# Two zero products a slot on TensorE, between the value products and the transposes of a two-layer attention kernel

## The chip, the cores and the metric

The kernel runs on one core of one Trainium2 chip. The metric is device time in microseconds (us), the median of several executions; lower is better.

## What is computed

The reference is two transformer blocks, one behind the other, on `x` of 8 batches, 128 tokens and 128 channels, all in float32. Each block has self-attention, cross-attention with a context `ctx_768` (8 x 128 x 96) and an MLP with four times 128 hidden channels; every one of the six sub-blocks starts with a layer norm that is scaled and shifted by the condition vector, and ends with a residual sum. The first block has 16 heads of 64 channels with rotary embedding. The second, where the change lies, has 16 heads of 8 channels:

```python
def _attend(q, k, v):
    sim = jnp.einsum('bhid,bhjd->bhij', q, k) * HD ** (-0.5)
    attn = jax.nn.softmax(sim, axis=-1)
    out = jnp.einsum('bhij,bhjd->bhid', attn, v)
    return out.transpose(0, 2, 1, 3).reshape(out.shape[0], -1, D)
...
h1 = _modulate(_ln(x), sh_msa, sc_msa)
...
x = x + (out @ W_proj + b_proj)
```

## The kernel before

Each engine has a program of its own, written out by hand, and the engines meet at counted semaphores. The order of instructions on each engine is the order of the code; there is no scheduler. SBUF tensors are allocated once, and PSUM is used as eight fixed banks of 128 x 512 float32: `S[0]`, `S[1]` and `X` (scores, in turn), `T[0]` and `T[1]` (transposed probabilities), `Y`, `W` (norm transposes, projections, sums) and `O` (value products).

Work is cut into items. An item is two heads of four batches (a half), so that one bank holds four 128 x 128 squares. A layer has 4 runs (self-attention of half 0 and 1, cross-attention of half 0 and 1) of 8 items, so 32 items. The first layer runs as slots -2 to 31 of `l0_slot`, the second as slots 0 to 39 of `l1_slot`, one item a slot, in a software pipeline that spans three slots. Every engine has a function of the same name with its own part of each slot. In slot s of the second layer:

- TensorE computes the scores of item s (`score1`, line 873 by way of the helper `mm`, shown as `bank<-km,q`: eight products with 32 rows of weights), then the value products of item s-2 (`prob_values1`, `bank<-swp,vst`), then transposes the probabilities of item s-1 into `T[0]` and `T[1]` (`transpose_probs1`, line 1139, `bank<-small,raw`), then does what `background1` has for the slot: `turn_back` (line 1170), `attention_T` (line 1176), `project_attention`, `transpose_norm` (line 884), or parts of the MLP. `score1` of slot s waits for the exponentials of the first head of item s-1.
- VectorE takes the row maxima (line 772) of both heads, copies `T[0]` to SBUF (line 777), and does statistics, sums and divisions.
- ScalarE computes the exponentials (line 506), four instructions a head, and between the two heads copies `T[1]` (line 512); in every fourth slot it also copies `O` (line 516).
- GpSimd masks keys and does part of the layer norms.

In slots 8, 16 and 24 a new run begins: there TensorE does the value products and transposes first, and the scores only after the projection of the new queries. In slots 12, 20 and 28 `project_attention` adds the attention's output, which VectorE then adds to `x`.

`keep_warm(count, dst)` issues `count` products of `idle`, a 128 x 512 bf16 tensor that VectorE sets to zero at the start, into the bank `dst`. Before the change it is called twice, ahead of the first layer, with 11 and 8 products. A product of it has 128 x 128 weights and 512 columns, and no semaphore.

Of the kernel before, what the change touches and what calls it, by code (L numbers as in the profile page):

```python
# [52 lines left out]
def place(s):  # L53

    return s // (2 * RUN), s // RUN % 2, s % RUN


def build(nc, small_in, x_in, ctx_in, ctxT_in, wqkv_in, wo_in, wmod_in, wsq_in, wff_in, row_in, out):
    es = ExitStack()
    with es:  # L60
# [64 lines left out]
        S, T, X, Y, O, W = bank[0:2], bank[2:4], bank[4], bank[5], bank[6], bank[7]  # L125
# [13 lines left out]
        def bcols(u):  # L139
            return slice(u * P, (u + 1) * P)  # L140
# [730 lines left out]
        def _(pe):  # L871
            def mm(o, lhsT, rhs, start, stop):
                return nc.tensor.matmul(o, lhsT, rhs, start=start, stop=stop, skip_group_check=True)  # L873

            def keep_warm(count, dst):
                for _ in range(count):
                    mm(dst[:, :], idle[:, 0:P], idle[:, :], True, True)
# [69 lines left out]
            def transpose_probs(s, hh):  # L947
                pe.wait_ge(norms[hh], s + 1)
                if s:
                    pe.wait_ge(copied[hh], s)  # L950
                if hh:
                    pe.wait_ge(v_out, min(s + 3, ITEMS))
                    if s == 28:
                        pe.wait_ge(gelu_done, FF)
                    if s == 31:
                        pe.wait_ge(vst_out[0], 1)
                for u in range(HALF):
                    last = nc.tensor.transpose(T[hh][:, bcols(u)], prob[:, hh, bcols(u)], ident)  # L958
                last.then_inc(probs_T[hh], 1)

            def prob_values(s):
                for hh in range(2):
                    pe.wait_ge(copied[hh], s + 1)
                if s:
                    pe.wait_ge(o_out, s)
                if s == 1:
                    wait_hT(0, 1)
                if s in (4, 5):
                    pe.wait_ge(ctx_h, s - 3)
                if 6 <= s <= 11:  # L970
                    pe.wait_ge(proj_out, s - 5)
                if s in (12, 20):
                    wait_hT(1, s // RUN - 1)
                if s == 13:
                    pe.wait_ge(mod_read, 2)
                if s == 27:
                    wait_hT(2, 0)
                if s == 28:
                    pe.wait_ge(x_sum[0], 3)
                for u in range(HALF):  # L980
                    for hh in range(2):
                        last = mm(O[DH0 * hh:DH0 * (hh + 1), bcols(u)],
                                  v0[:, s % 4, u * P + DH0 * hh:u * P + DH0 * (hh + 1)], probT[:, s % 2, hh, bcols(u)],
                                  True, True)
                last.then_inc(pv, 1)

            def project_out(s):
                a, half, n = place(s)
                if n == 0:
                    if s:  # L990
                        run = s // RUN - 1
                        pe.wait_ge(x_sum[run % 2], run // 2 + 1)
                    seed("ca_bo" if a else "sa_bo", W)
                    pe.wait_ge(ld_wo[a], 16)
                pe.wait_ge(o_out, s + 1)
                for u in range(HALF):
                    last = mm(W[:, bcols(u)], oT[:, s % 2, bcols(u)], wo[:, a * RUN + n, :], False, False)
                last.then_inc(wo_done, 1)

            def project_values(half):  # L1000
                dst = (T[1], Y)[half]
                if half:
                    pe.wait_ge(proj_out, AT["q", 1] + 1)
                else:
                    pe.wait_ge(copied[1], 31)
                for u in range(HALF):
                    last = mm(dst[:, bcols(u)], hT[:, half, bcols(u)], wsq[:, SQ["v"] * P:(SQ["v"] + 1) * P], True, True)
                last.then_inc(proj_v, 1)

            def project(what, half):  # L1010
                i = AT[what, half]
                dst = PROJ_BANK[i]
                if i == 0:
                    pe.wait_ge(ld_sq, 16)
                    pe.wait_ge(ld_ctxT, 16)
                if what in ("ck", "cv"):
                    pe.wait_ge(proj_out, AT["ctx1", half] + 1)
                if what == "q":
                    wait_hT(3, half)
                if what == "cq":  # L1020
                    wait_hT(4, half)
                weights = wsq[0:DC if what == "ctx1" else P, SQ["ctx" if what == "ctx1" else what] * P:][:, 0:P]
                src = {"ctx1": ctxT, "ck": ctx1T, "cv": ctx1T}.get(what, hT)
                if what == "cv":
                    for u in range(HALF):
                        last = mm(dst[:, bcols(u)], src[:, half, bcols(u)], weights, True, True)
                else:
                    last = mm(dst[:, :], weights, src[:, half, :], True, True)
                last.then_inc(proj, 1)
# [83 lines left out]
            def score1(s):  # L1113
                a, half, n = place(s)
                j = n // 2
                if n == 0:
                    pe.wait_ge(proj_out, AT["cq" if a else "q", half] + 1)
                    pe.wait_ge(km_first[half], a + 1)
                elif n % 2 == 0:
                    pe.wait_ge(km_rest[half], (SLOTS - 1) * a + j)  # L1120
                if s >= 1:
                    pe.wait_ge(exps1[0], s)
                if s >= 2:
                    pe.wait_ge(exps1[1], s - 1)
                for u in range(HALF):
                    for hh in range(2):
                        g = (2 * n + hh) % GROUPS
                        lanes = slice(GR * g, GR * (g + 1))
                        ins = mm(SB[(2 * s + hh) % 3][:, bcols(u)], q1[lanes, half, bcols(u)], km[lanes, half, j, bcols(u)],
                                 True, True)  # L1130
                        if u == HALF - 1:
                            ins.then_inc(scores1[hh], 1)

            def transpose_probs1(s, hh):
                pe.wait_ge(exps1[hh], s + 1)
                if s:
                    pe.wait_ge(copied1[hh], s)
                for u in range(HALF):
                    last = nc.tensor.transpose(T[hh][:, bcols(u)], prob1[:, s % 2, hh, bcols(u)], ident)  # L1139
                last.then_inc(probs_T1[hh], 1)  # L1140

            def prob_values1(s):
                a, half, n = place(s)
                for hh in range(2):
                    pe.wait_ge(copied1[hh], s + 1)
                if n == 0:
                    pe.wait_ge(vst_out[half], a + 1)
                if s == 0:
                    pe.wait_ge(o_out, ITEMS)
                if s % 4 == 0 and s:  # L1150
                    pe.wait_ge(os_out, s // 4)
                for u in range(HALF):
                    for hh in range(2):
                        c = (u * H + 2 * n + hh) * VW
                        last = mm(O[VW * u:VW * (u + 1), bcols(s % 4)], vst[:, half, c:c + VW], probT1[:, s % 2, hh, bcols(u)],
                                  hh == 0, hh == 1)
                last.then_inc(pv1, 1)
# [35 lines left out]
            def l1_slot(s):  # L1193
                first = s in (RUN, 2 * RUN, 3 * RUN)
                if s < ITEMS and not first:
                    score1(s)
                if s == 0:
                    transpose_probs(ITEMS - 1, 1)
                    project_out(ITEMS - 2)
                    prob_values(ITEMS - 1)  # L1200
                if first and s > RUN:
                    project("cq", s // RUN - 2)
                if 2 <= s <= ITEMS + 1:
                    prob_values1(s - 2)
                if 1 <= s <= ITEMS:
                    transpose_probs1(s - 1, 0)
                    transpose_probs1(s - 1, 1)
                if s == RUN:
                    project("q", 1)
                    project("k", 1)  # L1210
                if first:
                    score1(s)
                if s == RUN:
                    project_values(1)
                background1(s)
# [129 lines left out]
```

## Time and profile before

| | us |
|---|---|
| median of 3 runs | 428.16 (425.07 to 430.17) |
| profiled execution, its own time | 422.87 |
| its span, first to last instruction | 420.7 |
| TensorE busy | 383.0 |
| VectorE busy | 312.4 |
| ScalarE busy | 303.6 |
| GpSimd busy | 165.6 |
| TensorE's mean granted clock | 0.984 of full |

The time of an execution is 2.17 us more than its span. The second layer's slots begin at about 262 us and its last slots, which are MLP work, end with the span. "Busy" for TensorE comes from records whose ends are modelled, so the start times of its instructions are read rather than their ends. A float32 product of 128 x 128 shows as two records, a transpose as one. The granted clock is a share of 2.4 GHz; 0.50 is the lower of its two levels, 1.2 GHz, and a value between is a stretch that has some of both.

### The profile page before, as it was taken

The page shows a single profiled execution, that of the slowest core. Times are in us where ns is not written, and L with a number is a line of the kernel's source. Part 1 is how long each engine was busy: PE and PEld are TensorE (multiplying, and loading weights), DVE is VectorE, ACT ScalarE, POOL GpSimd, SP SyncE. Part 2 cuts the span into 40 slices and gives each one's busy share as a digit, 9 for nine tenths or more (in the row PEclk, how much of TensorE's full clock was granted, in tenths as well). Part 3 has the DMA queues.
Part 4 walks back from the last instruction along what each step waited for, and adds up shares of the span by engine and source line. Part 5 has one row for each costly group of instructions (what it writes and reads, how often), then busy time and mean ns, then how long its engine had stood idle before and what let it go on. Part 6 is the DMA issues. An engine that isn't in the chain of part 4 may idle for free. (4 is left out here: it accounts for less than half of the span.)

```text
span 420.7 us, 9918 instructions
## 1 busy us (share of the span) xinstructions
PE 383.0 (91%) x3599; PEld 288.5 (69%) x3599; DVE 312.4 (74%) x677; ACT 303.6 (72%) x1042; POOL 165.6 (39%) x159
## 2 busy tenths in 40 slices
PE   7778989999999999999999989899798898898976
PEld 3446767777877777777767577777586686687554
DVE  4699898988887999988999477764567567567430
ACT  2376777886885878787868947797698778688722
POOL 4578593523643443733346241321473402002020
PEclk9899999999999999999999999999999989989989
DMA  6334424232252121212221010000000000000000
GB/s 189 119 131 127 157 89 163 83 115 96 74 191 107 64 89 68 85 63 90 75 77 68 34 51 2 2 2 0 2 2 2 3 2 2 2 2 2 2 25 26
DMA packets 16036, 26.11 MB, mean 62 GB/s; under 512 B 3614, under 2 KB 6308, under 8 KB 15860
## 3 DMA queue, kind: packets, MB, share of 16 engines
q1 hardware_dynamic: 13572, 18.43, 12.2%
q0 software_dynamic: 1696, 6.16, 5.1%
q10 hardware_dynamic: 720, 0.87, 0.7%
q8 instruction: 30, 0.49, 0.5%
q14 instruction: 18, 0.15, 0.1%
HBM read 8.15 MB, written 0.52 MB: 21 GB/s over the span
## 5 line engine op out<-in xcount | busy, mean ns | idle before, releaser
L281 POOL TENSOR_TENSOR swp<-swp,small 128x512 f32<-128x512 f32 x64 | 82.0, 1293 | 108.2 <-PE bank L873 76.5
L411 ACT ACTIVATE prob<-bank,nmax 128x128 f32<-128x128 f32 x256 | 91.5, 391 | 4.8 <-DVE nmax L668 4.8
L506 ACT ACTIVATE raw<-bank,nmax 128x128 f32<-128x128 f32 x256 | 73.5, 391 | 20.1 <-DVE nmax L772 20.1
L772 DVE TENSOR_REDUCE nmax<-bank 128x4 f32<-128x512 f32 x64 | 41.2, 686 | 26.5 <-PE bank L873 26.3
L411 ACT ACTIVATION_READ_ACCUMULATOR prob<-bank,nmax 128x1 f32 x256 | 59.3, 231 | 0.0
L668 DVE TENSOR_REDUCE nmax<-bank 128x4 f32<-128x512 f32 x64 | 41.2, 685 | 17.7 <-PE bank L873 17.6
L222 POOL TENSOR_TENSOR rstd<-vare,neg_half 128x4 f32<-128x4 f32 x12 | 12.4, 1034 | 104.5 <-DVE vare L613 104.4
L675 DVE TENSOR_TENSOR prob<-prob,rz 128x512 f32<-128x512 f32 x64 | 49.9, 780 | 2.2
L873 PE MATMUL bank<-hT,wqkv 128*128 128x512 f32 x96 | 50.0, 606 | 1.1 <-ACT hT L394 1.1
L417 ACT ACTIVATE probT<-bank 128x512 f32<-128x512 f32 x32 | 19.1, 597 | 40.4 <-PE bank L958 40.4
L873 PE MATMUL bank<-km,q 32*128 32x128 f32 x512 | 37.5, 284 | 10.7 <-ACT raw L506 6.1
L958 PEld LDWEIGHTS bank<-small,prob 128*128 128x128 f32 x256 | 28.8, 140 | 25.9 <-DVE prob L675 15.7
L691 DVE TENSOR_TENSOR qk<-qk,swp 128x512 f32<-128x512 f32 x64 | 44.4, 733 | 2.4 <-issue 1.2
L958 PE MATMUL bank<-small,prob 128*128 128x128 f32 x256 | 40.5, 280 | 4.4 <-DVE prob L675 4.1
L685 DVE TENSOR_TENSOR qk<-bank,small 128x512 f32<-128x512 f32 x64 | 43.6, 681 | 1.0 <-ACT raw L402 0.9
L873 PEld LDWEIGHTS bank<-km,q 32*128 32x128 f32 x512 | 31.5, 187 | 17.8 <-ACT raw L506 7.6
L873 PE MATMUL bank<-qk 64*128 64x128 f32 x512 | 37.9, 288 | 5.9 <-DVE qk L691 5.9
L402 ACT ACTIVATE raw<-bank 128x512 f32<-128x512 f32 x64 | 40.7, 636 | 2.5 <-PE bank L873 2.5
L873 PEld LDWEIGHTS bank<-wo,oT 128*128 128x128 f32 x256 | 32.9, 191 | 13.0 <-issue 11.9
L873 PEld LDWEIGHTS bank<-qk 64*128 64x128 f32 x512 | 31.8, 190 | 12.1 <-DVE qk L691 6.9
L873 PE MATMUL bank<-probT,v 128*64 128x128 f32 x512 | 35.0, 278 | 3.9 <-ACT hT L394 1.8
L1139 PE MATMUL bank<-small,raw 128*128 128x128 f32 x256 | 36.9, 289 | 0.1
(112 smaller groups left out, 649.3 us busy)
## 6 DMA issues: line engine op xcount, KB each, us to landing
swp<-raw SPq DMA_DIRECT2D x128, 128.0 KB, 2.1
wqkv<-in_wqkv POOLq DMA_DIRECT2D x13, 192.0 KB, 3.0
wo<-in_wo POOLq DMA_DIRECT2D x2, 512.0 KB, 5.1
wff<-in_wff POOLq DMA_DIRECT2D x1, 1024.0 KB, 5.6
wsq<-in_wsq POOLq DMA_DIRECT2D x1, 576.0 KB, 6.2
x<-in_x SPq DMA_DIRECT2D x2, 256.0 KB, 4.6
wmod<-in_wmod POOLq DMA_DIRECT2D x1, 512.0 KB, 4.2
out_x<-x SPq DMA_DIRECT2D x2, 256.0 KB, 2.3
```

What stands on the lines that cost most here:

```text
L281: nc.gpsimd.tensor_tensor(four(swp[:, m % 2, f, :]), four(swp[:, m % 2, f, :]), sin[f], ALU.mult).then_inc(rope_sin[f], 1)
L402: nc.scalar.activation(raw[:, m % 2, f, :], (X, Y)[f][:, :], ACT.Copy).then_inc(raw_out[f], 1)
L411: last = nc.scalar.activation(prob[:, hh, bcols(u)], S[hh][:, bcols(u)], ACT.Exp, bias=nmax[:, s % 2, hh, u:u + 1], accum_out=zsum[:, s % ...
L506: last = nc.scalar.activation(prob1[:, s % 2, hh, bcols(u)], SB[(2 * s + hh) % 3][:, bcols(u)], ACT.Exp, bias=nmax[:, s % 2, hh, u:u + 1])
L668: nc.vector.tensor_reduce(nmax[:, s % 2, hh, :], four(S[hh][:, :]), AX.X, ALU.max, negate=True).then_inc(rowmax[hh], 1)
L675: nc.vector.tensor_tensor(four(prob[:, hh, :]), four(prob[:, hh, :]), rz[:, s % 2, hh, :].unsqueeze(2).broadcast_to([P, HALF, P]), ALU.mul ...
L685: nc.vector.tensor_tensor(four(qk[:, m % 2, f, :]), four((X, Y)[f][:, :]), cos[f], ALU.mult).then_inc(rope_cos[f], 1)
L691: nc.vector.tensor_tensor(qk[:, m % 2, f, :], qk[:, m % 2, f, :], swp[:, m % 2, f, :], ALU.add).then_inc(roped[f], 1)
L772: nc.vector.tensor_reduce(nmax[:, s % 2, hh, :], four(SB[(2 * s + hh) % 3][:, :]), AX.X, ALU.max, negate=True).then_inc(rowmax1[hh], 1)
L873: return nc.tensor.matmul(o, lhsT, rhs, start=start, stop=stop, skip_group_check=True)
L958: last = nc.tensor.transpose(T[hh][:, bcols(u)], prob[:, hh, bcols(u)], ident)
L1139: last = nc.tensor.transpose(T[hh][:, bcols(u)], prob1[:, s % 2, hh, bcols(u)], ident)
```

## The change

Slots 2 to 33 of the second layer get one more line on TensorE:

```diff
@@ -1202,6 +1202,7 @@
                     project("cq", s // RUN - 2)
                 if 2 <= s <= ITEMS + 1:
                     prob_values1(s - 2)
+                    keep_warm(2, T[0])
                 if 1 <= s <= ITEMS:
                     transpose_probs1(s - 1, 0)
                     transpose_probs1(s - 1, 1)
```

That is 32 calls and 64 products. They write `T[0]`, whose last content has been copied by then, since `prob_values1(s - 2)` in front of them waits for that copy; the transposes behind them overwrite it. No wait and no semaphore is added, and no other engine's program changes.

TensorE in slots 10 and 11 before (`bank<-km,q` are scores, `bank<-swp,vst` value products, L1139 the transposes of probabilities, L1170 `turn_back`, L1176 `attention_T`):

```order
L873 MATMUL bank<-km,q 128x128 x8
L873 MATMUL bank<-swp,vst 32x128 x8
L1139 MATMUL bank<-small,raw 128x128 x8
L1170 MATMUL bank<-small,oS 128x128 x4
L873 MATMUL bank<-km,q 128x128 x8
L873 MATMUL bank<-swp,vst 32x128 x8
L1139 MATMUL bank<-small,raw 128x128 x8
L1176 MATMUL bank<-small,xn 128x128 x4
```

The same two slots on TensorE now:

```order
L873 MATMUL bank<-km,q 128x128 x8
L873 MATMUL bank<-swp,vst 32x128 x8
L873 MATMUL bank<-idle 128x512 x2
L1139 MATMUL bank<-small,raw 128x128 x8
L1170 MATMUL bank<-small,oS 128x128 x4
L873 MATMUL bank<-km,q 128x128 x8
L873 MATMUL bank<-swp,vst 32x128 x8
L873 MATMUL bank<-idle 128x512 x2
L1139 MATMUL bank<-small,raw 128x128 x8
L1176 MATMUL bank<-small,xn 128x128 x4
```

The transposes and all that follows them in the slot stand behind two more products; the scores of the next slot too.

TensorE at the start of a run, slots 15 to 17, before (`bank<-hT,wsq` is the projection of the new queries; the x16 are the scores of slots 16 and 17):

```order
L1170 MATMUL bank<-small,oS 128x128 x4
L873 MATMUL bank<-hT,wsq 128x512
L873 MATMUL bank<-swp,vst 32x128 x8
L1139 MATMUL bank<-small,raw 128x128 x8
L873 MATMUL bank<-km,q 128x128 x16
L873 MATMUL bank<-swp,vst 32x128 x8
L1139 MATMUL bank<-small,raw 128x128 x8
```

And now:

```order
L1170 MATMUL bank<-small,oS 128x128 x4
L873 MATMUL bank<-hT,wsq 128x512
L873 MATMUL bank<-swp,vst 32x128 x8
L873 MATMUL bank<-idle 128x512 x2
L1139 MATMUL bank<-small,raw 128x128 x8
L873 MATMUL bank<-km,q 128x128 x16
L873 MATMUL bank<-swp,vst 32x128 x8
L873 MATMUL bank<-idle 128x512 x2
L1139 MATMUL bank<-small,raw 128x128 x8
```

Between the scores of slot 16 and those of slot 17 stands nothing, as before.

## Rows read from the trace of the kernel before

**Rows 1.** The page: TensorE's busy time, and the clock granted in 40 slices.

```profile
PE 383.0 (91%) x3599; PEld 288.5 (69%) x3599; DVE 312.4 (74%) x677; ACT 303.6 (72%) x1042; POOL 165.6 (39%) x159
...
PEclk9899999999999999999999999999999989989989
```

**Rows 2.** The chain that ended last, stretches of slots 9 to 13: start, us, what.

```profile
306.84 1.02 PE bank L1139 x8
307.87 0.38 issue
308.25 1.75 PE bank L873 x32
```

**Rows 3.** Windows: stretch and length, busy us (instructions) by engine, PEclk, DMA, GB/s.

```profile
305.09:308.25 3.16, 2.78 (x41) 2.25 (x41) 1.89 (x3) 2.77 (x11) 3.16 (x3) 1.00 0.00 0
308.25:311.39 3.14, 3.14 (x45) 2.65 (x45) 1.91 (x3) 3.14 (x11) 3.14 (x3) 1.00 0.02 5
326.44:332.06 5.62, 5.62 (x71) 4.18 (x71) 3.79 (x9) 4.34 (x14) 4.73 (x4) 1.00 0.02 6
332.06:335.17 3.11, 1.16 (x17) 0.97 (x16) 1.65 (x3) 1.79 (x6) 0.00 (x0) 1.00 0.00 0
335.17:339.24 4.07, 4.07 (x41) 3.19 (x41) 1.98 (x3) 2.13 (x8) 0.74 (x2) 0.62 0.00 0
339.24:342.63 3.39, 3.36 (x45) 2.84 (x45) 1.98 (x3) 3.29 (x11) 0.00 (x0) 0.95 0.02 5
366.01:370.18 4.17, 4.17 (x41) 3.23 (x41) 1.98 (x3) 2.12 (x8) 0.00 (x0) 0.61 0.00 0
```

**Rows 4.** Timeline of TensorE, slot 10: start, us, operation, count [idle before].

```profile
308.25 1.16 PE L873 MATMUL bank<-km,q 32*128 32x128 f32 x16 [0.38 <-issue]
309.33 0.67 PE L873 MATMUL bank<-swp,vst 128*32 128x128 f32 x16
309.93 1.09 PE L1139 MATMUL bank<-small,raw 128*128 128x128 f32 x8
310.86 0.60 PE L1170 MATMUL bank<-small,oS 128*128 128x128 f32 x4
```

**Rows 5.** Timeline of ScalarE and VectorE, slot 10.

```profile
308.97 2.30 ACT L506 ACTIVATE raw<-bank,nmax 128x128 f32<-128x128 f32 x8
309.41 1.29 DVE L772 TENSOR_REDUCE nmax<-bank 128x4 f32<-128x512 f32 x2 [1.24 <-PE bank L873]
```

**Rows 6.** Timeline of TensorE: the groups of the second layer that begin after a wait.

```profile
273.05 1.16 PE L873 MATMUL bank<-km,q 32*128 32x128 f32 x16 [0.88 <-ACT raw L506]
276.18 0.63 PE L884 MATMUL bank<-small,xn 128*128 128x128 f32 x4 [0.36 <-DVE xn L621]
293.34 1.16 PE L873 MATMUL bank<-km,q 32*128 32x128 f32 x16 [0.45 <-ACT raw L506]
322.37 1.16 PE L873 MATMUL bank<-km,q 32*128 32x128 f32 x16 [0.93 <-issue]
325.88 0.63 PE L884 MATMUL bank<-small,xn 128*128 128x128 f32 x4 [0.73 <-DVE xn L621]
335.17 1.20 PE L873 MATMUL bank<-km,q 32*128 32x128 f32 x16 [1.95 <-ACT raw L506]
356.71 0.63 PE L884 MATMUL bank<-small,xn 128*128 128x128 f32 x4 [0.33 <-DVE xn L621]
391.91 0.67 PE L873 MATMUL bank<-swp,vst 128*32 128x128 f32 x16 [0.48 <-ACT swp L512]
```

**Rows 7.** Timeline of TensorE: bf16 products of 512 columns, and what follows one.

```profile
5.90 1.89 PE L873 MATMUL bank<-idle 128*128 128x512 bf16 x8
...
317.26 0.38 PE L873 MATMUL bank<-parts_row,ones 3*128 3x512 bf16 x1
317.57 1.16 PE L873 MATMUL bank<-wsq,oT 128*128 128x128 f32 x8
```

**Rows 8.** The tile `idle`: weight loads and products, shortest/median/longest in ns.

```profile
L873 PEld LDWEIGHTS bank<-idle x19: 95/117/181, 1.3 to 7.2; 128*128 128x128 bf16 x19
L873 PE MATMUL bank<-idle x19: 376/380/634, 1.3 to 7.4; 128*128 128x512 bf16 x19
```

## The prediction

> **What bounds the kernel now.** I read the page first: TensorE is busy 91% of the span, and its clock is nearly always full [rows 1]. That says little of one stage, so I went to the second layer's slots, from 262 us on, the only ones that change: the chain of waits, then TensorE's timeline with the waits ahead of each group, then windows cut at the starts of the scores.
>
> A plain slot takes 3.14 to 3.16 us, and two things come out alike in it. In slot 9 (305.09 to 308.25) TensorE has scores, value products and transposes, 2.78 us of work, and then waits 0.38 us [rows 2, 3]: here a loop sets the pace (scores 1.1 us, row maximum of the first head half of 1.29, its exponentials half of 2.30 [rows 4, 5]; with handovers about 3.1 us), since the next scores need those exponentials. In slot 10 four transposes of `turn_back` are added, and TensorE runs from one score to the next without a wait, 3.14 us, scores, values, transposes, `turn_back` each starting where the former's pace allows [rows 3, 4]. ScalarE is full in that slot as well, 3.14 us. So wherever a slot has anything beside its three standing groups, TensorE's queue is the path; where it has not, or where VectorE's sum and statistics hold back the row maxima, TensorE waits.
>
> **The change part by part.** Nothing is removed, no wait is added, no transfer moves. Added are 64 bf16 products of 512 columns.
>
> Price of a pair. The zero products ahead of the first layer are the same instruction. The eight at 5.90 us take 1.89 us, of which the last takes 0.38, so the seven steps between starts are (1.89 - 0.38) / 7 = 0.216 us each at full clock [rows 7, 8]. The 0.117 us weight load of each [rows 8] is inside that step. A pair is 0.43 us. The value products before and the transposes behind are separated by a changeover already; I take it to be paid once, as now. The other end: a lone bf16 product in this layer, the seed of a sum, delays what follows by 317.57 - 317.26 = 0.31 us [rows 7]; two such are 0.62. Below 0.43 a pair can't go at this clock, since products don't overlap in these rows, but its effect on the path can, down to zero, where TensorE waits afterwards. I take 0.43, from the row that shows the very instruction.
>
> Now slot by slot, by the wait that follows the pair [rows 6]:
> - Full price, 18 slots. TensorE runs without a wait behind the pair: 4 and 5 (MLP work), 8 (projections), 10 to 12, 15 and 16 (326.44 to 332.06 is 5.62 us of 5.62 busy [rows 3]), 18 to 20, 23 and 24, 26 to 28, 32 and 33 (MLP work again). 18 x 0.432 = 7.78 us.
> - Slots 9, 17, 25: the wait of 0.38 us takes the pair but for 0.05: 0.15 us.
> - Slots 3 and 7 wait 0.36 us for normalised rows before their norm transpose, which leaves 0.07 each: 0.14. Slots 22 and 30 wait 0.33 there, and leave 0.10 each: 0.20.
> - Slot 31: 0.48 us of wait for ScalarE's copy of the transposes, which the pair itself makes later. Between 0 and 0.43, I take 0.20.
> - Nothing in slots 2 (0.88 of wait), 6 (0.45), 13, 21, 29 (0.93, behind VectorE's residual sum and statistics) and 14 (0.73). If that cover were gone it would be 6 x 0.43 = 2.6 us.
>
> Sum 7.78 + 0.15 + 0.14 + 0.20 + 0.20 = 8.47 us. The transposes are 0.43 later in every slot, and with them ScalarE's copy, which sits between its two heads' exponentials. In slot 10 it would push the second head by a few tenths, but the next scores are later too, by 0.43, so ScalarE isn't the end of the path there.
>
> Ends of the sum. Low: TensorE's ends are modelled, and ScalarE is full in slot 10. If ScalarE were the true bound in the six slots like it (10, 11, 18, 19, 26, 27), the pair would cost nothing there: 8.47 - 2.59 = 5.9 us. High: a pair of 0.62 is 18 x 0.62 = 11.2, plus 2.4 in the others by the same waits, 13.6 us.
>
> The clock. It fell twice in this layer. Scores of slot 17 came 1.95 us after TensorE went idle [rows 6], and from them on the clock shows 0.62 and then 0.95 [rows 3], so it was at the 1.2 GHz level for most of a slot; the same at 366.01. The two slots took 4.07 and 3.39 us where 3.14 is the pace at full clock: 0.93 + 0.25 = 1.18 us; at 366.01 it is 1.03 + 0.25 = 1.28, so 2.4 us together. Do the pairs mend that? They stand before the transposes, and the wait lies between the scores of slot 16 and of slot 17, with nothing of the change in it. It stays as long as it is, so I expect falls as before, and count zero for the clock. A fall that comes with the pairs in place costs a little more, since they run at half speed too.
>
> The Trainium skill ("TensorE: Matmul & The Clock Gate", "A second HAM failure mode: psum-queue depth-cycling") holds that many short idles between groups of products can make the clock swing. By that rule filling TensorE's time anywhere would help. The trace speaks against it here: slots with waits of 0.38 us kept 1.00, and the fall came behind the one wait of 1.95 us. By the rule the sum would lose the 2.4 us of both falls; by the rows it loses nothing.
>
> **Against which time.** The profiled execution took 422.87 us, so its sum is 431.3. The runs had a median of 428.16, 5.3 us more, from 425.07 to 430.17. What they lose over the profiled one I can't see. The added work is the same in both, so I put the forecast at 428.16 + 8.47 = 436.6 us, 2.0% slower. A measurement of this kernel tells about 1% (4.3 us) from no change.
>
> **Rivals.**
> 1. The clock is what the pairs buy, in part. The four or so slots around a fall have more busy time, and both falls go: 436.6 - 2.4 = 434.2 us. For it: the falls are next to pairs. Against: the wait itself stays. 13%.
> 2. Faster or even, by the same clock but at a larger size. If the 5.3 us by which the runs exceed the profiled execution were falls in this layer too (four or five at 1.2), the pairs would do away with them all: -2.4 - 5.3 = -7.7 us, against 5.9 to 8.5 us of added work: 426.4 to 429.0 us. It decides from some seven falls a run on (8.47 / 1.2); the profile has two in the layer. For it: the runs vary by 5 us, as a clock would make them. Against: the falls would have to be where a pair reaches. 7%, and 4% for beyond 1% faster.
> 3. ScalarE bounds more than TensorE: 5.9 us of cost, 434.1 us. For it: 3.14 us busy of 3.14. Against: TensorE's starts follow each other without a wait in the same slots, and slots 15 and 16, with 5.62 us of 5.62, have ScalarE at 4.34 [rows 3]. 10%.
> 4. A pair costs as the seed product does, 0.62: 441.8 us. For it: changing between column-tiled products, bf16 and float32 has a price that eight equal products don't show. 12%.
> 5. The pairs don't delay at all since TensorE could run ahead. Its queue is in order, and the transposes that follow have their inputs long before; nothing speaks for it. Under 1%.
>
> **How the numbers follow.** Forecast 58%, rivals 13, 7, 10 and 12%. Its own range is 433 to 440. The whole range reaches from rival 3 with part of rival 1 (5.9 - 2.4 = 3.5, 431.7 us), less a microsecond for the scatter of a median, to rival 4: 430.5 to 441.5. Faster by over 1% 4% (rival 2's far end); within 1% (up to 432.4) 14%, from the rest of rival 2, and where rivals 1 and 3 meet; slower by over 1% 82%.
>
> **What would show it.** In the changed profile: 64 more bf16 products of `idle` with 0.216 us between the two of a pair; slots 10 to 12 at about 3.57 us instead of 3.14, back to back; slot 9 at 3.2; slots 13 and 14 as long as now; the stretch of slots 15 and 16 at 6.5 instead of 5.62; a wait of about 1.95 us still ahead of slot 17's scores, and some of these waits still followed by a clock of 0.5 to 0.6. A run of eight slots would be some 2.3 us longer. I would be wrong if slots 10 to 12 keep 3.14 us (rival 3), if more than 0.5 us lies between the last value product and the first transpose beyond what lies there now (rival 4), or if the layer shows fewer falls of the clock and a time under 432 (rivals 1, 2).

## The result, and the profile after

| | before | changed |
|---|---|---|
| median of 20 runs each, us | 427.03 | 430.39 |
| lowest to highest, us | 421.03 to 430.17 | 426.58 to 434.49 |
| ratio, 95% interval | | 1.0125 (1.0087 to 1.0163) |
| profiled execution: span, us | 420.7 | 429.5 |

The change makes the kernel slower, by 1.25% in the ratio (5.3 us) and by 3.4 us between the medians. The ratio leaves out the longest runs of either kernel as disturbed; since in the kernel before these are mostly the runs with the lowest clock, and the clock is part of the question, I use medians, means over all runs and the trace beside it. The two profiled spans differ by 8.8 us, more than either: 2.07 of it are there before the second layer's third slot (269.39 us before, 271.46 after), in code that is the same in both. That part is scatter: the same slot begins at 270.31 us in a second trace of the kernel before and at 269.06 in a second one of the changed kernel.

The page of the changed kernel, the two rows that answer to [rows 1]:

```profile
PE 392.2 (91%) x3646; PEld 294.9 (69%) x3663; DVE 316.0 (74%) x677; ACT 305.6 (71%) x1042; POOL 165.2 (38%) x159
...
PEclk9889999999999999999999999999999999999999
```

TensorE is busy 9.2 us more, 91% again. The low clocks have moved: more of them in slices 2 and 3, in the first layer, fewer later.

Windows of the changed kernel, cut at the scores as in [rows 3]: slots 9, 10, 11, 12, then 15 with 16's transposes, the wait ahead of slot 17, slots 17, 18, and 25.

```profile
308.36:311.51 3.15, 2.99 (x41) 2.44 (x43) 1.68 (x3) 2.66 (x10) 3.15 (x3) 1.00 0.00 0
311.51:315.24 3.73, 3.61 (x48) 2.89 (x47) 2.29 (x4) 3.48 (x11) 3.73 (x3) 1.00 0.02 4
315.24:318.77 3.53, 3.37 (x47) 2.85 (x47) 2.83 (x6) 2.77 (x10) 1.29 (x3) 1.00 0.00 0
318.77:323.27 4.50, 4.50 (x53) 3.47 (x52) 1.98 (x3) 4.31 (x15) 0.00 (x0) 1.00 0.01 4
...
331.03:337.43 6.40, 6.24 (x74) 4.57 (x74) 3.88 (x9) 4.72 (x16) 4.73 (x4) 1.00 0.02 5
337.43:340.54 3.11, 1.16 (x17) 0.97 (x16) 1.66 (x3) 1.79 (x6) 0.00 (x0) 1.00 0.00 0
340.54:344.86 4.32, 4.02 (x41) 3.22 (x42) 1.98 (x3) 2.12 (x8) 0.74 (x2) 0.71 0.00 0
344.86:348.79 3.93, 3.93 (x47) 3.25 (x46) 1.98 (x3) 3.58 (x11) 0.00 (x0) 0.89 0.02 4
...
373.71:376.86 3.15, 2.99 (x41) 2.44 (x43) 1.68 (x3) 2.11 (x8) 0.00 (x0) 1.00 0.00 0
```

Read by length. Slot 9 is as long as before (3.15 for 3.16): its wait has swallowed the pair whole. Slot 11 has 0.37 more (3.16 before), slot 12 0.39 (4.11), the stretch of slots 15 and 16 0.78 (5.62). Slot 10 has 0.59 more, the odd one. The clock fell behind the wait that ends at 340.54, as it had before behind the one that ends at 335.17, but at slot 25 it stayed at 1.00, where before it fell.

There is a third fall in the layer, in both kernels, which the prediction did not count: in the MLP work behind slot 31, after two waits of 1.12 to 1.13 and 1.10 us. TensorE's timeline of the kernel before, then the same group of products in the changed kernel, then in a kernel without any fall in the layer ("The wait itself filled", below):

```profile
406.09 0.63 PE L884 MATMUL bank<-small,xn 128*128 128x128 f32 x4 [1.13 <-POOL xn L229]
407.82 5.37 PE L873 MATMUL bank<-hT,wff 128*128 128x512 f32 x8 [1.10 <-ACT hT L394]
...
416.56 5.37 PE L873 MATMUL bank<-hT,wff 128*128 128x512 f32 x8 [1.10 <-ACT hT L394]
...
403.98 3.67 PE L873 MATMUL bank<-hT,wff 128*128 128x512 f32 x8 [1.10 <-DVE hT L630]
```

At full clock the group takes 3.67 us in place of 5.37, so this fall costs 1.7 us in either. The 148.9 us that the first expectation below gives for the layer without its two falls still has this one inside; at full clock it is 147.2.

TensorE's timeline, the start of slots 10 to 12:

```profile
311.51 1.16 PE L873 MATMUL bank<-km,q 32*128 32x128 f32 x16
312.79 0.67 PE L873 MATMUL bank<-swp,vst 128*32 128x128 f32 x16
313.39 0.61 PE L873 MATMUL bank<-idle 128*128 128x512 bf16 x2
313.83 1.04 PE L1139 MATMUL bank<-small,raw 128*128 128x128 f32 x8
314.71 0.60 PE L1170 MATMUL bank<-small,oS 128*128 128x128 f32 x4
315.24 1.16 PE L873 MATMUL bank<-km,q 32*128 32x128 f32 x16
```

The pair takes 313.83 - 313.39 = 0.44 us to the first transpose, as forecast, but the transposes then take 0.88 us to the start of `turn_back`, where it was 0.93 (309.93 to 310.86 in [rows 4]). That is why a full slot pays 0.37 to 0.39 and not 0.43.

The odd slot: value products begin 1.28 us after the scores, where it was 1.08. ScalarE's timeline shows why:

```profile
311.56 0.60 ACT L512 ACTIVATE swp<-bank 128x512 f32<-128x512 f32 x1
312.05 0.59 ACT L516 ACTIVATE oS<-bank 128x512 f32<-128x512 f32 x1
312.53 2.17 ACT L506 ACTIVATE raw<-bank,nmax 128x128 f32<-128x128 f32 x8
```

The pair makes the transposes of slot 9 later, ScalarE's copy of them (311.56) with them, and behind that copy stands, in every fourth slot, the copy of bank `O`, which ends at 312.64. The value products of slot 10 write `O`, and wait for it.

The tile `idle` in the changed kernel:

```profile
L873 PEld LDWEIGHTS bank<-idle x83: 95/98/181, 1.3 to 403.4; 128*128 128x128 bf16 x83
L873 PE MATMUL bank<-idle x66: 376/379/634, 1.3 to 403.6; 128*128 128x512 bf16 x66
```

83 weight loads are 19 + 64: all pairs ran. Only 66 products have a record, so where the timeline shows one product with 0.16 us of idle time ahead, a record is missing.

### The profile page after: what moved, and what is told of

The parts are those of the page before. It is cut to its first block and busy times, and to the rows that moved or that the text cites. A ratio compares the mean times of both kernels' runs of the same rounds, so it can differ in the third digit from the quotient of the medians.

```text
span 429.5 us, 10029 instructions
## 1 busy us (share of the span) xinstructions
PE 392.2 (91%) x3646; PEld 294.9 (69%) x3663; DVE 316.0 (74%) x677; ACT 305.6 (71%) x1042; POOL 165.2 (38%) x159
## 5 line engine op out<-in xcount | busy, mean ns | idle before, releaser
L506 ACT ACTIVATE raw<-bank,nmax 128x128 f32<-128x128 f32 x256 | 72.6, 379 | 19.9 <-DVE nmax L772 19.4
L675 DVE TENSOR_TENSOR prob<-prob,rz 128x512 f32<-128x512 f32 x64 | 51.3, 801 | 2.2
L691 DVE TENSOR_TENSOR qk<-qk,swp 128x512 f32<-128x512 f32 x64 | 45.3, 748 | 2.3 <-issue 1.2
L873 PEld LDWEIGHTS bank<-qk 64*128 64x128 f32 x512 | 32.0, 191 | 11.2 <-DVE qk L691 5.8
L1139 PEld LDWEIGHTS bank<-small,raw 128*128 128x128 f32 x256 | 30.7, 144 | 6.7 <-issue 0.5
```

The costliest lines, as they stand in the source:

```text
L506: last = nc.scalar.activation(prob1[:, s % 2, hh, bcols(u)], SB[(2 * s + hh) % 3][:, bcols(u)], ACT.Exp, bias=nmax[:, s % 2, hh, u:u + 1])
L675: nc.vector.tensor_tensor(four(prob[:, hh, :]), four(prob[:, hh, :]), rz[:, s % 2, hh, :].unsqueeze(2).broadcast_to([P, HALF, P]), ALU.mul ...
L691: nc.vector.tensor_tensor(qk[:, m % 2, f, :], qk[:, m % 2, f, :], swp[:, m % 2, f, :], ALU.add).then_inc(roped[f], 1)
```

## The experiments

Two questions: does a pair cost what the sum says, slot by slot; and if it does, 7.8 us at full clock (below), why do the medians differ by 3.4 only? My theory for the second, formed from the result: the pairs give clock back, and the first trace of the kernel before, with two short falls behind the waits of 1.95 us, was a lucky one. The rival: the pairs cost less in undisturbed executions than in the profiled one.

All runs stand against the kernel before on the same chip. "Mean clock" is the granted clock, averaged over the runs of a kernel.

| kernel | median us | ratio (95%) | mean us | mean clock |
|---|---|---|---|---|
| before (with the first four) | 425.8 | | 426.2 | 0.974 |
| pairs in the covered slots | 426.9 | 1.0029 (0.9984 to 1.0075) | 426.6 | 0.978 |
| pairs in the full slots | 434.2 | 1.0141 (1.0029 to 1.0253) | 433.2 | 0.970 |
| four products a place | 441.7 | 1.0402 (1.0330 to 1.0473) | 441.9 | 0.985 |
| wait filled, 8, no pairs | 419.0 | 0.9888 (0.9836 to 0.9941) | 419.0 | 0.994 |
| before (with the second four) | 427.0 | | 426.5 | 0.972 |
| all pairs, wait filled | 427.7 | 1.0081 (1.0032 to 1.0129) | 427.6 | 0.993 |
| pairs on both sides of the wait | 424.9 | 0.9982 (0.9933 to 1.0032) | 425.0 | 0.983 |
| wait filled, 4, no pairs | 419.8 | 0.9890 (0.9807 to 0.9972) | 420.1 | 0.993 |
| six waits filled, no pairs | 419.0 | 0.9861 (0.9794 to 0.9927) | 419.2 | 0.995 |
| before (with the third four) | 427.0 | | 426.9 | 0.974 |
| pairs behind the wait only | 427.9 | 1.0018 (0.9981 to 1.0056) | 427.5 | 0.976 |
| pairs ahead of the wait only | 427.3 | 1.0014 (0.9977 to 1.0050) | 427.3 | 0.972 |
| before, once more | 427.6 | 1.0006 (0.9967 to 1.0046) | 427.3 | 0.972 |
| all pairs (the change), once more | 429.6 | 1.0071 (1.0038 to 1.0104) | 429.9 | 0.986 |

"The stretch" below is from the scores of slot 2 to the end of the span, which leaves the first layer out. "The two waits" are those of 1.95 us ahead of the scores of slots 17 and 25.

**Pairs only where TensorE waits.**

```diff
-                    keep_warm(2, T[0])
+                    if s in (2, 3, 6, 7, 9, 13, 14, 17, 21, 22, 25, 29, 30, 31):
+                        keep_warm(2, T[0])
```

> Pairs only in the 14 slots that the prediction counts as covered or nearly (2, 3, 6, 7, 9, 13, 14, 17, 21, 22, 25, 29, 30, 31); the other 18 slots as before. Slot theory (a pair costs where TensorE has no wait behind it): the stretch from the scores of slot 2 to the end of the program, 151.3 us before (148.9 without its two falls of the clock), grows by 0.2 to 0.7 us at equal clock; the time is within 0.3% of before. Flat theory (every pair costs the same 0.24 us, 7.8 / 32): the stretch grows by 3.4 us, the time by 0.8%. Clock theory (filling steadies the clock wherever it stands): fewer falls a run than before, and a time 1 to 3 us under before.

Measured: slots 2, 3, 6, 9, 13, 14, 21, 22, 29 and 30 as long as before to 0.01 us. Slot 7, up to the scores of slot 8, has 0.25 more, slot 10 0.19 (the copy of `O`), slot 31 to the end 0.28 more than where no clock fell, and slots 18 and 26, each behind a slot with a pair and a due copy of `O`, should have slot 10's 0.19 too: 1.1 us in all, above what I expected, and far from the 3.4 of the flat theory. The time is that of before. The clock theory in its plain form finds no support: with 14 pairs the clock still falls behind both of the two waits, and the mean clock, 0.978 against 0.974, is higher by less than the runs can tell (0.0035, give or take 0.005).

**Pairs only where it doesn't.** The same line with `if s not in`.

> Pairs only in the 18 slots that the prediction counts at full price. Slot theory: the stretch from slot 2 grows by 7.2 to 7.8 us at equal clock, as it does with all 32 pairs, and the time is that of the changed kernel, some 5 us over before. Flat theory: the stretch grows by 4.4 us. In both, slot 10 and slot 26, whose predecessors 9 and 25 have no pair now, take 3.53 us as slot 11 does, not 3.73.

Measured: slots 11, 12 and 15 with 16 pay as in the changed kernel, to 0.01 us, and slot 10 takes 3.53 us, as expected without a pair in slot 9. The stretch is 162.2 us; slots 17, 18, 25 and 26 and the part from slot 31 on are 1.8, 2.2, 0.6, 2.0 and 1.7 us longer than where no clock fell, so 153.9 at full clock, 6.7 over the 147.2 of the kernels that have no fall in it. 1.1 + 6.7 = 7.8, the price of all pairs. The mean time was 7.0 us over before, not 5, with a mean clock of 0.970, no better than before's. That fits a kernel that pays its price in full, but these are six runs with a wide spread, and the ratio, 1.0141 (1.0029 to 1.0253), leaves anything from 1 to 11 us: a hint of what the pairs do together, not a proof.

**Twice as many products.** `keep_warm(4, T[0])`.

> Four products in each of the 32 places in place of two. Slot theory: another 0.43 us in the 18 full slots (7.8), and the covers of 0.33 to 0.48 us are used up in the others, so 3.5 to 4 us more there: the stretch from slot 2 grows by 11 to 12 us over the changed kernel at equal clock, by 19 to 20 over before; time some 17 us over before. If products of zeros were partly free on the path (their price being the changeover), the stretch would grow by under 8. Clock theory: the falls of the clock in this layer get fewer still.

Measured: the stretch is 167.9 us with one fall of 1.6 in it, so 166.2: 11.2 over the changed kernel at full clock, 19.0 over before. Slot 11 grows by another 0.43 (3.96), slot 9 by 0.38 (3.53), slot 13 by nothing (3.71), as the waits say. The second pair costs 0.43, without the 0.05 discount of the first. The mean time is 15.7 us over before, so here too some 3 us of the 19.0 come back (give or take 3), with a mean clock of 0.985 against 0.974.

**The wait itself filled, and no pairs.**

```diff
                 if first:
                     score1(s)
                 if s == RUN:
                     project_values(1)
+                if s in (2 * RUN, 3 * RUN):
+                    pe.wait_ge(o_norm, 2 * (s // RUN) - 1)
+                    keep_warm(8, Y)
```

> No pairs. Eight products of zeros into Y behind the scores of slots 16 and 24, in the wait of 1.95 us ahead of the scores of slots 17 and 25 (8 x 0.216 = 1.73 us). Theory that the falls come from that wait: the two falls at slots 17 and 25 are gone in every look, slots 17 and 18 take 3.15 and 3.2 us, nothing is delayed, and the median is 0.5 to 2.4 us under before. Rival (the falls come from elsewhere, from the low share of work in small products): falls remain, time as before or a little over it.

TensorE's timeline of this kernel, slots 16 to 18, and its windows of slots 17, 18 and 25:

```profile
330.67 1.16 PE L873 MATMUL bank<-km,q 32*128 32x128 f32 x16
331.76 1.90 PE L873 MATMUL bank<-idle 128*128 128x512 bf16 x8
333.78 1.16 PE L873 MATMUL bank<-km,q 32*128 32x128 f32 x16
```

```profile
333.78:336.93 3.15, 2.78 (x40) 2.25 (x41) 1.89 (x3) 2.21 (x9) 0.74 (x2) 1.00 0.00 0
336.93:340.08 3.15, 3.15 (x45) 2.66 (x45) 1.91 (x3) 3.15 (x11) 0.00 (x0) 1.00 0.02 5
363.45:366.61 3.16, 2.78 (x41) 2.26 (x41) 1.89 (x3) 2.22 (x9) 0.00 (x0) 1.00 0.00 0
```

The scores of slot 17 start 3.11 us after those of slot 16, exactly as without the products, and no clock falls in the layer. The same holds in the other three kernels below that fill these waits (eight waits in four traces, no fall), so the wait is the cause of both falls. The gain is more than the 0.5 to 2.4 us that I expected: the mean is 7.2 us below before, the ratio says 4.8. The six runs agree within 2.7 us (417.3 to 420.0) where before's 17 spread over 11. A part of before's scatter is therefore the clock behind these two waits, but not all of it: twelve runs of the next kernel, with the same waits filled, spread over 6.8, and the first layer alone varies by 4 us between traces (slot 2 begins at 268.0 to 272.2).

**All pairs, and the wait filled.** The diff above on top of the changed kernel.

> The changed kernel with its 32 pairs, and the eight products in the waits ahead of slots 17 and 25 as well. Price theory (the pairs cost 7.8 us of TensorE's time, and the smaller difference measured, 3.4 to 5.3 us, is what they give back of the clock): with the falls gone in both, the difference to the kernel with the gap products alone (419.0 us) is 7.5 to 8.5 us, so 426.5 to 427.5 us. Rival (the pairs delay by less than that in undisturbed executions): 422 to 424.5 us.

Windows of slots 9, 10, 11, and 15 with 16:

```profile
306.60:309.76 3.16, 3.16 (x42) 2.45 (x43) 1.68 (x3) 2.67 (x10) 3.16 (x3) 1.00 0.00 0
309.76:313.48 3.72, 3.61 (x47) 2.89 (x47) 2.28 (x4) 3.47 (x11) 3.72 (x3) 1.00 0.02 4
313.48:317.01 3.53, 3.53 (x47) 2.85 (x46) 2.83 (x6) 2.77 (x10) 1.31 (x3) 1.00 0.00 0
...
329.28:335.68 6.40, 6.40 (x76) 4.57 (x75) 3.89 (x9) 4.72 (x15) 4.72 (x4) 1.00 0.02 5
```

The same lengths as in the changed kernel, now with no fall anywhere in the layer, the MLP work at its end included. The stretch is 155.0 us against 147.2 with the wait filled and no pairs: the price of the change at full clock is 7.8 us. The times say the same: 427.7 against 419.0, 8.7 us, 0.2 above the range that I gave; against the kernel with four products in the wait it is 7.5 between the means. The rival (422 to 424.5) is out.

**Pairs beside the waits: both sides, behind, ahead.** `if s in (16, 17, 18, 24, 25, 26)`, then `(17, 18, 25, 26)`, then `(16, 24)`, ahead of the same `keep_warm(2, T[0])`.

> Pairs only in slots 16, 17, 18 and 24, 25, 26, so beside the two waits of 1.95 us. Price at full clock by the slot theory: 0.39 in 16, 0 in 17, 0.4 to 0.6 in 18, twice: 1.6 to 2.0 us. If the pairs beside the waits are what gives clock back, the mean clock is near the changed kernel's 0.986 and the mean time 424 to 425 us (1 to 2 under before's 426.2). If it takes all pairs (or they give nothing, and the changed kernel had luck), the mean clock stays near 0.974 and the time is 427.5 to 429 us.

> Pairs only in the two slots behind each of the waits of 1.95 us (17, 18, 25, 26). Price at full clock, from the looks so far: 0 in 17 and 25, 0.57 in 18 and 26, so 1.1 us over the gap kernels' 419 to 420. If pairs behind the wait are what gives clock back (a fall ends sooner with more work behind it), the falls are short, the mean clock is near 0.983 as with pairs on both sides, and the time 423 to 424.5 us. If it is those ahead: clock near 0.973, time 427 to 428 us.

> Pairs only in slots 16 and 24, ahead of each wait. Price at full clock 0.39 each, 0.8 us. If pairs ahead of the wait give clock back (the clock doesn't fall, or not as often): mean clock near 0.983, 423 to 424 us. If it is those behind: clock near 0.973, falls that last over both of the slots 17 and 18 or 25 and 26, 426.5 to 427.5 us.

On both sides: mean clock 0.983 and 425.0 us, as expected if the pairs next to the waits do the work. The clock is clear of before's (0.011 higher, give or take 0.005), the time is not (1.5 us lower, give or take 1.8). Pairs behind alone: 0.976 and 427.5 us. Pairs ahead alone: 0.972 and 427.3 us. Both are hardly to be told from before, and in clock and time each run gave the answer that I had written down for "it is the other side". So neither side does it alone; it takes both.

**Four in the wait in place of eight.** `keep_warm(4, Y)` in the diff above.

> No pairs; four products in place of eight in the waits ahead of slots 17 and 25, so that about 1.1 us of each wait stays empty. Theory that it is the length of the empty stretch that lets the clock fall: a wait of 1.1 us is no longer than those of other slots that kept the full clock, so the falls are gone here too: 418.5 to 420 us. Rival (the whole wait has to be filled): part of the falls come back, 421 to 424 us.

```profile
332.97 1.04 PE L873 MATMUL bank<-idle 128*128 128x512 bf16 x4
335.00 1.16 PE L873 MATMUL bank<-km,q 32*128 32x128 f32 x16 [0.98 <-ACT raw L506]
```

A wait of 0.98 us is left, and the clock stayed full: 419.8 us. Half the filling is enough. That does not make the length of the wait the rule, as my expectation had it. A wait of 1.35 us stands ahead of the scores of slot 8 in every kernel here, and the clock fell behind it in none of 14 traces:

```profile
302.00 1.16 PE L873 MATMUL bank<-km,q 32*128 32x128 f32 x16 [1.35 <-ACT k L434]
```

The waits of 1.13 and 1.10 us ahead of the last MLP, which are shorter, had a fall behind them in 7 of the 13 traces in which they were not filled. So length alone does not decide.

**Four more waits filled.** Products ahead of the first layer's scores and round the last norm, beside those of slots 16 and 24.

```diff
             transpose_norm(0, 0, [T[0], T[1]])
+            keep_warm(4, O)
...
+                if s == 0:
+                    keep_warm(10, O)
                 score(s)
...
+                        if run == 3:
+                            keep_warm(4, O)
                         transpose_norm(4 + run // 2, half, [Y, W])
+                        if run == 3:
+                            keep_warm(4, O)
```

> The gap products of slots 16 and 24, and products of zeros in four more waits outside the attention slots: 4 behind the first norm's transposes, 10 ahead of the first layer's first scores (a wait of 2.84 us), and 4 before and 4 behind the last norm's transposes (waits of 1.1 us each). If the falls in the first layer (18 to 24 us) and in the tail (408 us) come from these waits, they go as well: another 1 to 3 us under the gap kernel, 416 to 418 us. If they don't, or if the products delay what follows them: 419 to 421 us.

419.0 us: no more than the two waits alone give. In its trace the clock is low in the first layer from about 24 to 30 us, where no wait was filled. In the tail there was little to win: the three kernels with the two waits filled and the tail left alone show no fall there, though seven of the ten traces with the two waits unfilled do. Why filling slots 17 and 25 should go with that is open.

**Both kernels once more.**

> The kernel before once more, for a second look at its falls and its clock. If the profiled execution (two falls of 1.2 us each) was a lucky one, this look shows a longer fall (2 us or more over slots 17 and 18, or 25 and 26) and the mean clock of its runs is 0.970 to 0.976 again, against 0.984 in the first look. Rival (the falls always cost 1.2 us): slots 17+18 and 25+26 sum to 7.5 us at most.

Windows of the kernel before in this second trace: the wait ahead of slot 17, slots 17 and 18, then the same of slots 25 and 26.

```profile
332.96:336.08 3.12, 1.17 (x18) 0.97 (x17) 1.66 (x3) 1.80 (x6) 0.00 (x0) 1.00 0.00 0
336.08:339.66 3.58, 3.58 (x40) 2.93 (x41) 1.98 (x3) 2.12 (x8) 0.74 (x2) 0.73 0.00 0
339.66:345.04 5.38, 5.38 (x46) 4.60 (x45) 1.98 (x3) 3.60 (x11) 0.00 (x0) 0.55 0.01 3
365.30:368.41 3.11, 1.16 (x17) 0.97 (x16) 1.65 (x3) 1.79 (x6) 0.00 (x0) 1.00 0.02 5
368.41:373.35 4.94, 4.94 (x41) 4.00 (x41) 1.98 (x3) 2.13 (x8) 0.00 (x0) 0.50 0.00 0
373.35:378.94 5.59, 5.59 (x45) 4.81 (x44) 1.98 (x3) 3.81 (x12) 0.00 (x0) 0.52 0.01 3
```

The falls last over both slots: 8.96 and 10.53 us where 6.3 is the pace at full clock, so 2.7 and 4.2 us, against 1.2 and 1.3 in the trace that the prediction had [rows 3]. Its span is 425.9 us, 5.2 more than that trace's 420.7; 4.3 of it are in the stretch and 0.9 in front of it.

> The changed kernel once more, beside its base on the same chip. Ratio 1.007 to 1.013, mean clock 0.984 to 0.987, and falls that cost at most 1.4 us each (slots 17+18 or 25+26 at most 8.3 us, where 6.9 is full clock). If a fall of over 2 us shows up, the account that the pairs shorten the falls is weaker.

```profile
338.14:342.70 4.56, 4.56 (x42) 3.26 (x42) 1.98 (x3) 2.13 (x8) 0.74 (x2) 0.65 0.01 4
342.70:346.49 3.79, 3.72 (x48) 3.00 (x47) 1.98 (x3) 3.49 (x11) 0.00 (x0) 0.97 0.00 0
371.40:374.56 3.16, 3.16 (x42) 2.45 (x43) 1.68 (x3) 2.12 (x8) 0.00 (x0) 1.00 0.00 0
374.56:378.28 3.72, 3.61 (x48) 2.89 (x47) 2.28 (x4) 3.48 (x11) 0.00 (x0) 1.00 0.02 4
```

Again one fall in place of two behind the two waits, over 8.35 us where 6.9 is full clock: 1.5 us, a tenth more than I had allowed. The fall in the tail is there too, 1.7 us. The ratio is 1.0071, at the low end of what I expected, and the mean clock 0.986.

All traces with the two waits unfilled, counted together. I drew the groups after seeing them:

| | traces | waits with a fall behind them | falls that last through the second slot (over 5.3 us) | what a fall costs, us |
|---|---|---|---|---|
| pairs on both sides (change twice, four a place, beside the waits) | 4 | 4 of 8 | none of 4 | 1.4 to 1.6 |
| pairs behind only | 1 | 2 of 2 | none of 2 | 1.6, 2.7 |
| not in both slots behind (before twice, covered, full, ahead only) | 5 | 10 of 10 | 5 of 10 | 1.1 to 4.5 |

The cost is that of slots 17 with 18, or 25 with 26, over their length at full clock. One trace a kernel is a thin sample: that of the kernel with pairs on both sides (421.96 us) and that of pairs ahead only (423.21) are among the fastest of their twelve runs. The mean clocks in the table of kernels stand on all runs.

## Why the prediction was right, and where it was not

The direction was right, and so was the mechanism of the price; the clock was not. Forecast were 8.47 us, 2.0%; measured were 1.25% and 0.7% in two series, 5.3 and 3.0 us. The forecast of 436.6 us lay 6 us above the median that came, and the lower end of the range, 430.5, just above it; with the ratio on the median that the prediction started from it is 433.5 us, inside. Of the 6.2 us between 436.6 and the median of 430.39, 1.1 are the starting time (428.16 by three runs, 427.03 by twenty), 0.7 the price of the pairs and some 4.4 the clock that they give back. That the range held at all is partly luck: its low end stood on ScalarE taking 2.6 us off the price, which it did not do, and on a clock that gives back 2.4 us, where it gave more.

**The price of a pair.** 0.43 us by the row of the eight products: right as the time to the first transpose (0.44), and 0.05 too much as a price on the path (0.37 to 0.39). The 18 slots come to 6.7 us in place of 7.78, since slot 8 paid only 0.17. Rival 4, a pair of 0.62, is out.

**Full and covered slots.** Right in nearly every slot, but for one term missed and small leftovers. Slots 3, 9, 17, 22, 25 and 30: I charged 0.42 together, and each paid 0.01 or less. The likely reason is that a pair moves what follows it by 0.39 and not 0.43, and that the idle time that the trace gives is measured from a modelled end. Slots 7 and 8 were charged 0.50 and paid 0.42 together: 0.25 by the pair in slot 7, where I had 0.07 and where the value products of slot 8 now wait 0.18 us for ScalarE's delayed copy, and 0.17 by the pair in slot 8, where I had 0.43. I had also said that TensorE runs without a wait behind that pair, and it waits 1.35 us ahead of the scores. Slot 31 paid 0.28 for my 0.20. Missed: the copy of bank `O` behind the delayed copy of `T[1]`, 0.2 us in each of slots 10, 18 and 26. I had looked at ScalarE's queue there and asked only whether the exponentials come late, not who waits for the instruction between them. 6.7 + 0.25 + 0.28 + 0.6 = 7.8 us at full clock for 8.47; the terms too high and the term missed partly cancel, which is luck.

**Rival 3** (ScalarE bounds slots 10 and 11) fell: slots 11, 19 and 27 paid 0.37 each, and slot 10 even more.

**"Count zero for the clock"** is the step that failed. Its premise held: the wait of 1.95 us stayed as long as it was. What I drew from it did not. (It also counted two falls where the trace had three; the third, 1.7 us in the MLP work at the end, is there in both traces of both kernels and so does not enter the difference.) With the wait filled the two kernels lie 8.7 us apart (427.6 and 419.0), unfilled 3.2 (430.1 and 426.9, means of the change's two series and of before's third). So by the means the falls cost the kernel before some 7.9 us a run and the changed one 2.5, and about 5 us of the price come back as clock. By the ratios it is 3 to 5 us: they put the two kernels 5.3 and 3.0 us apart. Rival 1 had the mechanism and about half the size, since it priced a fall by the one trace that I had: 1.2 us, where the second shows 2.7 and 4.2. Rival 2 guessed rightly that most of the 5.3 us between the profiled execution and the median were falls in this layer (4.3 of 5.2 us in the second trace), and wrongly that pairs would do away with all of them.

**The skill's rule** (the Trainium skill, "TensorE: Matmul & The Clock Gate", "A second HAM failure mode: psum-queue depth-cycling": many short idles can make the clock swing) I had set aside because slots with waits of 0.38 us kept the full clock. That reading stands for the short waits: filling them with 14 pairs changed neither the time nor, as far as the runs can tell, the clock. But work beside a long wait does count, which I had not allowed for. The same page ("What's actually happening") says that the gate follows how busy the PE has been recently; read that way, the neighbourhood of the wait matters and not its length alone, and the run with pairs on both sides agrees, with a clock of 0.983 against the 0.972 of the kernel before.

What stays open is why it takes both sides. With pairs in both slots behind the wait none of six falls lasts through the second slot, though one of them still costs 2.7 us; with pairs on both sides there are falls at half of the waits only. These are counts from ten traces, and no run measured the activity that the chip sees.

## What to carry to other kernels

Filler products cost nearly their full time wherever the engine's queue is the path, and nothing where a long enough wait follows and no other engine's work is held up by them: read the wait behind each place, and who waits for the work that they delay, before putting them there. If the clock falls behind a wait, fill that wait and no other place: four or eight products in each of two waits gave 1.1%, 64 products spread over the slots lost 0.7 to 1.25%. Don't price a fall of the clock by one profiled execution, and ask for the granted clock of many runs before taking it as a constant.

## What the runs showed of the hardware

- One wait of 1.95 us on TensorE, with small products on either side, is enough for the clock to drop to 1.2 GHz (behind both such waits in both traces of the kernel before); 0.98 us left of it was not, in the one trace of that kernel. The length is not all: behind a wait of 1.35 us the clock fell in none of 14 traces, behind two waits of 1.13 and 1.10 us in 7 of 13. How long the low level then lasts varies from one execution to the next for the same code: 1.2, 2.7 and 4.2 us lost behind the same waits. Pairs of products on both sides of the waits raise the mean clock from 0.972 to 0.983; on one side only (0.976, 0.972) they don't by more than the runs can tell.
- A bf16 product of 512 columns on zeros, amid float32 work, costs 0.216 us at full clock, its weight load hidden, and the eight transposes that follow such a pair take 0.88 us to what follows them in place of 0.93.
- The version with the two waits filled is faster than both kernels: 419.0 us, ratio 0.989 (0.984 to 0.994) to the kernel before.
